# First attention: a quarter of each chunk's values done one step later, and the heads copied in one piece

## What is computed

```
h = layer_norm(x, ln1_g, ln1_b)
q, k, v = split(h @ w_qkv.T)                 # 16 heads of 16
# chunks of 128 queries; keys: the chunk before and the own one
scores = (q . kcat) / 4
scores = where((j >= i + 1) & (j <= i + 128) & valid, scores, -inf)
attn = softmax(scores)
x = x + (attn @ vcat) @ w_o.T
```

## Time and profile before

| | |
|---|---|
| median of 3 runs (lowest, highest) | 1763.08 us (1760.52, 1764.54) |
| the profiled execution | 1759.69 us |
| its span in the profile | 1757.9 us, and 1.8 us around it |
| PE, DVE, ACT, POOL busy | 96%, 82%, 67%, 60% |
| first attention | from the start to about 370 us |
| granted clock of PE from 40 to 370 us | 1.00 |

### The profile page before, as it was taken

How to read it: one execution, slowest core, us unless ns; L and a number is a source line. 1 busy time by engine, 2 the same in 40 slices (tenths; PEclk the granted TensorE clock), 3 DMA queues, 4 the chain that set the end, 5 groups by cost and what they waited for, 6 DMA issues and landing times.

```text
span 1757.9 us, 43282 instructions
## 1 busy us (share of the span) xinstructions
PE 1695.5 (96%) x15168; PEld 1460.7 (83%) x15168; DVE 1446.6 (82%) x3686; ACT 1170.4 (67%) x3024; POOL 1052.0 (60%) x1052
## 2 busy tenths in 40 slices
PE   6999999989999999999998999999999999999997
PEld 4777777779998788888887888878888888888886
DVE  6888988868887999989997655579999999967776
ACT  6999888855544778878775343367787787743332
POOL 3676566534334687887774444367878777634333
PEclk9999999999999999999999999999999999999999
DMA  3111211022322322222223313122222222131221
GB/s 109 38 38 38 65 38 35 26 103 66 117 72 65 98 81 66 76 76 66 80 67 89 107 54 99 54 92 75 80 63 81 72 70 81 56 111 60 73 84 37
DMA packets 174626, 125.44 MB, mean 71 GB/s; under 512 B 20824, under 2 KB 173664, under 8 KB 173664
## 3 DMA queue, kind: packets, MB, share of 16 engines
q1 hardware_dynamic: 174432, 122.98, 23.0%
HBM read 88.32 MB, written 34.61 MB: 70 GB/s over the span
## 4 chain that ended last, share of the span: by engine, by line
PE 84%; DVE 9%; ACT 3%; issue 3%; DMA 1%; POOL 0%; SPq 0%; POOLq 0%; DVEq 0%; ACTq 0%
PE psum L612 18%; PE psum L614 17%; PE psum L613 17%; PE psum L948 6%; PE psum L916 5%; PE psum L929 5%; PE psum L727 3%; PE psum L709 3%; PE psum L890 3%; ACT a_probs L1757 2%; PE psum L662 1%; DVE a_neg_max L1240 1%; DVE psum L1238 1%; PE psum L699 1%; PE psum L1053 1%
## 5 line engine op out<-in xcount | busy, mean ns | idle before, releaser
L1876 ACT ACTIVATE b_probs<-masked,neg_max 128x256 f32<-128x256 f32 (+1 forms) x512 | 249.8, 489 | 119.4 <-DVE neg_max L1370 119.4
L612 PE MATMUL psum<-wa_hi,b_h_hi 128*128 128x512 f32 (+1 forms) x576 | 234.4, 407 | 6.0 <-DVE wa_lo L1167 3.6
L614 PE MATMUL psum<-wa_hi,b_h_lo 128*128 128x512 f32 (+1 forms) x576 | 214.1, 372 | 0.0
L613 PE MATMUL psum<-wa_lo,b_h_hi 128*128 128x512 f32 (+1 forms) x576 | 214.0, 372 | 0.0
L1370 DVE CUSTOM_DVE_ANT_0 masked<-psum,mask 128x256 f32<-128x256 f32 (+1 forms) x512 | 177.2, 412 | 41.1 <-PE psum L916 40.2
L612 PE MATMUL psum<-g_h_hi,wm_hi 128*128 128x512 f32 (+1 forms) x480 | 190.3, 397 | 3.5 <-POOL g_h_lo L2148 2.4
L2105 POOL TENSOR_TENSOR g_in<-g_in,minus_half 128x16 f32<-128x16 f32 x64 | 187.7, 2933 | 5.3
L614 PE MATMUL psum<-g_h_hi,wm_lo 128*128 128x512 f32 (+1 forms) x480 | 189.2, 394 | 0.0
L613 PE MATMUL psum<-g_h_lo,wm_hi 128*128 128x512 f32 (+1 forms) x480 | 189.2, 394 | 0.0
L1962 ACT ACTIVATE gate<-psum,vec_b 128x512 f32<-128x512 f32 x96 | 66.0, 687 | 153.6 <-PE psum L614 153.5
L612 PE MATMUL psum<-wm_hi,u_hi 128*128 128x256 f32 x576 | 164.5, 286 | 0.1
(11 more groups left out here) (167 smaller groups left out, 5432.6 us busy)
## 6 DMA issues: line engine op xcount, KB each, us to landing
b_inv_t<-inverse_rows SPq DMA_DIRECT2D x128, 128.0 KB, 3.0
x_mid<-y_out SPq DMA_DIRECT2D x96, 128.0 KB, 2.3
rope_in<-in_rope SPq DMA_DIRECT2D x64, 128.0 KB, 2.4
x_res<-x_state SPq DMA_DIRECT2D x64, 128.0 KB, 2.8
g_in<-x_mid SPq DMA_DIRECT2D x32, 256.0 KB, 3.7
w_raw<-in_w_mlp_b SPq DMA_DIRECT2D x2, 2154.0 KB, 9.1
x_in<-in_x SPq DMA_DIRECT2D x32, 128.0 KB, 2.2
x_res<-in_x SPq DMA_DIRECT2D x32, 128.0 KB, 2.2
```

The costliest lines, as they stand in the source:

```text
L612: nc.tensor.matmul(out, a_hi, b_hi, start=first, stop=False)
L613: nc.tensor.matmul(out, a_hi, b_lo, start=False, stop=False)
L614: return nc.tensor.matmul(out, a_lo, b_hi, start=False, stop=last)
L1876: ins = nc.scalar.activation(out, src, ACT.Exp, bias=neg_max[:, r, k:k + 1], scale=-1.0, accum_out=row_sum[:, n % 2, 4 * r + k:4 * r + k + 1])
```

## The change

values takes a tuple of tiles in place of p. Tile 0 of chunk n stays in step n; tile 1 (a quarter of the chunk's values) moves to step n+1, between project_qk and transpose_probs(4(n+1)). The last chunk (n = 31) keeps tiles 0 and 1 together. Tiles 2 and 3 stay where they were, but no longer wait for head_copied. pv_done is still raised twice a chunk, after tile 1 and after tile 3. copy_heads copies all 512 columns in one instruction at the place of the former second copy, head_copied counts one per chunk, and the waits for it are renumbered.

```diff
--- before.py
+++ after.py
@@ -106,6 +106,16 @@
 ...
+
+
+def a_early_tiles(n):
+
+    return (0, 1) if n == NCH - 1 else (0,)
+
+
+def a_late_tiles(n):
+
+    return (1,)
 
 
 def a_heads_bank(n):
@@ -709,28 +719,28 @@
                     mm = nc.tensor.transpose(W2[:, k * P:k * P + P], a_probs[:, i % 2, k, :], ident[:])
                 mm.then_inc(S["pt_ready"], 1)
 
-            def values(n, p):
-
-
-                if n + p > 0:
-                    pe.wait_ge(S["head_copied"], 2 * n + p)
-                if p == 0:
+            def values(n, tiles):
+
+                p = tiles[0] // 2
+                if tiles[0] == 0:
+                    if n > 0:
+                        pe.wait_ge(S["head_copied"], n)
                     pe.wait_ge(S["v_copied"], n + 1)
                     if a_chunk(n - 2):
                         pe.wait_ge(S["y_ready"], min(n - 1, NCH - 3))
                 pe.wait_ge(S["select_ready"], 4 * n + 2 * p + 2)
                 blocks = [(n, p_now)] if a_batch_first(n) else [(n - 1, p_before), (n, p_now)]
-                for j in range(2):
-                    t = 2 * p + j
+                for t in tiles:
                     for m, probs_of in blocks:
                         for g in range(4):
                             mm = nc.tensor.matmul(O[32 * g:32 * g + 32, t * P:t * P + P], v_aug[:, m % VRING, 4 * t + g, :],
-                                                  probs_of[:, 2 * p + g // 2, 2 * (g % 2) + j, :],
+                                                  probs_of[:, 2 * p + g // 2, 2 * (g % 2) + t % 2, :],
                                                   start=(m == blocks[0][0]), stop=(m == n), tile_position=(0, 32 * g))
-                mm.then_inc(S["pv_done"], 1)
+                if tiles[-1] % 2 == 1:
+                    mm.then_inc(S["pv_done"], 1)
 
             def transpose_heads(n):
-                pe.wait_ge(S["head_copied"], 2 * n + 2)
+                pe.wait_ge(S["head_copied"], n + 1)
                 pe.wait_ge(S["qt_ready"], min(n + 3, NCH))
                 if 0 < n < NCH - 1:
                     pe.wait_ge(S["o_lo"], n)
@@ -752,7 +762,7 @@
                 pe.wait_ge(S["o_hi"], n + 1)
                 pe.wait_ge(S["o_lo"], n + 1)
                 if n < NCH - 3:
-                    pe.wait_ge(S["head_copied"], 2 * n + 4)
+                    pe.wait_ge(S["head_copied"], n + 2)
                 else:
                     pe.wait_ge(S["pt_copied"], 4 * NCH)
                 if n > NCH - 3:
@@ -782,10 +792,12 @@
                     transpose_z(s + 2)
                 if a_chunk(s + 1) and s > -1:
                     project_qk(s + 1)
+                if a_chunk(s - 1):
+                    values(s - 1, a_late_tiles(s - 1))
                 if a_chunk(s):
                     transpose_probs(4 * s)
                 if a_chunk(s - 1):
-                    values(s - 1, 1)
+                    values(s - 1, (2, 3))
                 if a_chunk(s):
                     scores(s, 1)
                     transpose_probs(4 * s + 1)
@@ -800,7 +812,7 @@
                     transpose_k(s + 1)
                 if a_chunk(s):
                     transpose_probs(4 * s + 2)
-                    values(s, 0)
+                    values(s, a_early_tiles(s))
                 if a_chunk(s - 1) and s < NCH - 1:
                     transpose_heads(s - 1)
 
@@ -808,7 +820,7 @@
             pe_mlp(pe, MLP_A, MA, None, opening=0)
             out_project(NCH - 3)
             transpose_heads(NCH - 2)
-            values(NCH - 1, 1)
+            values(NCH - 1, (2, 3))
             transpose_o(NCH - 2)
             pe_mlp(pe, MLP_A, MA, None, opening=1)
             transpose_heads(NCH - 1)
@@ -1766,12 +1778,11 @@
                     a.wait_ge(S["pv_done"], 2 * (n - 1) + r // 2 + 1)
                 nc.scalar.activation(p_now[:, r, :, :].rearrange("p h q -> p (h q)"), W2[:], ACT.Copy).then_inc(S["pt_copied"], 1)
 
-            def copy_heads(n, p):
-                a.wait_ge(S["pv_done"], 2 * n + p + 1)
+            def copy_heads(n):
+                a.wait_ge(S["pv_done"], 2 * n + 2)
                 if n > 0:
                     a.wait_ge(S["out_steps"], 3 * n - 2)
-                at = slice(p * D, p * D + D)
-                nc.scalar.activation(head_t[:, at], O[:, at], ACT.Copy).then_inc(S["head_copied"], 1)
+                nc.scalar.activation(head_t[:], O[:], ACT.Copy).then_inc(S["head_copied"], 1)
 
             def o_high(n):
                 a.wait_ge(S["out_steps"], a_out_step(n, 1))
@@ -1780,13 +1791,10 @@
 
             for s in a_steps():
                 if a_chunk(s - 1):
-                    if s < NCH:
-                        copy_heads(s - 1, 0)
                     copy_probs(4 * s - 1)
                     if s == NCH:
                         act_mlp(a, MLP_A, MA, None, opening="gate")
-                        copy_heads(s - 1, 0)
-                        copy_heads(s - 1, 1)
+                        copy_heads(s - 1)
                 if a_chunk(s - 2) and s != NCH - 1:
                     o_high(s - 2)
                 if a_chunk(s):
```

## The result

| | before | changed |
|---|---|---|
| median of 10 runs each | 1762.46 us | 1767.59 us (1765.25 to 1769.1) |
| profiled execution, its span | 1759.69, 1757.9 us | 1765.25, 1763.5 us |
| a steady step of the first attention | 10.79 us | 11.00 us |

The changed kernel is slower: the ratio is 1.0028, 95% interval [1.0018, 1.0038], or +5.1 us. The forecast was +6.1 us and 1769.2, on a base of 1763.1.

What follows compares the result with a forecast made beforehand. PE bounds the kernel, but in the first attention's steps ACT's exponentials hold the scores; +7.2 us over the steps and -1.1 at the tail give +6.1 on 1763.1, so 1769.2 us; 8 in 10: 1762.5 to 1772.5.

Steps and rivals of the forecast that it cites:

- this case: The whole kernel gets slower: chance 0.77, forecast 1769.2 us, own range 1768 to 1772 us with the spread of runs.
- the second rival: Late values between project_qk and transposes cost no switching: +0.02 us a step, 1762.5 us; 15% for within 0.2%.
- The wait that takes the place of the work: Before scores(s+1, 0): 0.44 us of removed PE work becomes waiting, since scores need ACT's exponentials + 0.14; gain 0.
- the ring: One first-attention step as a loop: PE to the heads' transposes, then DVE and ACT, back to PE; 10.79 us a turn.
- The heads held by q_t: End of a step: the heads' transposes wait for finish_q_t, as in step 16 (q_t ends 200.71, heads start 200.81).
- The price of the insertion: Last project_qk matmul to round 0's transposes: 0.93 us against 0.66 with late values, +0.27 us a step (+0.24 to +0.30).
- The sum over the steps: Late values in s = 1 to 31, 26 of these steps at the full 0.27 us: +7.2 us (6.4 to 8.1).
- The copy of the heads: On ACT: one 128x512 copy of 0.60 us replaces two of 0.46, growing by 0.14 ahead of copy_probs(4s+1); cost 0.
- the cover: ACT's idle time ahead of copy_probs(4s+1): 0.26 us, and 0.27 more since PE comes later, hiding the wider copy's growth.
- the third rival: Wider heads copy ends after copy_probs(4s+1) could start: up to 0.14 us in 29 steps, +4.1, 1773.3 us; 5%.
- The tail: At values(31, second half): the wait for the first half's heads copy is dropped, PE gains 1.08 us; -1.1 us.
- The first rival: ACT doesn't hold the scores, so PE keeps 0.44 us a step: -0.14 to -0.20 a step, 1757.4 us total; 7%.

## Why the prediction was right, point by point

**The total.** The way and the mechanism were right, the size was not quite. The change was forecast as +6.1 us, from 5.3 to 7.0, and cost 5.1, which is below that range; 1767.59 also lies below the 1768 to 1772 given for this case. It lies within 1762.5 to 1772.5, but that range was drawn down for the second rival, which did not come. Of the 1.6 us between 1769.2 and 1767.59, 1.0 is the change and 0.6 the base, since ten runs of the kernel before have a median of 1762.46 where three had 1763.08.

**The wait that takes the place of the work.** Right, to 0.02 us. The step that decided the sign was to ask how far ACT's exponentials ended ahead of the scores (0.15 in the step that was read, 0.14 in most), and how near they could come (0.14, rows 6). All profiles with ACT on the ring show 0.14 to 0.15.

**The heads held by q_t.** Right: heads start 0.10 after q_t's end in the changed kernel, as they did after step 16. It costs nothing, since the scores' wait is longer.

**The price of the insertion.** Taken as 0.93, with 0.90 and 0.96 as bounds; it is 0.89 to 0.90. The rule from the recorded end (values start 0.07 before the end of what precedes them) holds behind a 512-wide matmul too: 318.32 + 0.39 = 318.71, and the values start at 318.64. So my way in of 0.385 was too long, and the middle was the wrong choice: the late values start 0.32 behind the last matmul of project_qk, under the 0.33 to 0.39 that I had named as a sign. The spacings are 0.09 us longer on the way in (318.32 to 318.64, less the usual 0.235) and 0.10 us on the way out (0.33 from last group to transposes, less 0.23). The Trainium skill's "TensorEngine Tiling", section "Tiling Modes", says that a change of mode drains TensorE. The trace agrees in that time is lost at both changes; that it is a drain, and not something else in which these matmuls differ, no run here shows. The Trainium skill's "TensorE: Matmul & The Clock Gate", Part 2, says that weight loads are pulled ahead of matmuls in flight, if the row groups don't conflict or the load goes to the background buffer. Whether any were pulled ahead here isn't shown; the 0.09 and 0.10 us remained, so the second rival's condition wasn't met.

**The sum over the steps.** Forecast +7.2, from 6.4 to 8.1. Measured between the heads of s = 1 and of s = 30: 313.38 us before, 318.94 after, +5.6. This is the term that was mis-sized: it fell below its lower bound, by the price of the insertion above and by step 29. A steady step grew by 0.22, not 0.27: 0.235 for the insertion less 0.01 to 0.02 at the scores, which I had rounded to nothing. 25 such steps give 5.5; s = 16 and 17 together 0.14. Step 29 became shorter by 0.11 (11.54 to 11.43) where I had counted a full 0.27. There DVE has the MLP's first statistics to do and runs without a break from the merging of the step's first scores to the end of y_out, 331.75 to 340.63 before and 338.36 to 347.25 after: 8.88 and 8.89 us. The late values stand beside that run and cost nothing. Ahead of it 0.17 us is lost (DVE starts 1.56 after the heads of s = 28 instead of 1.39, since the scores there are held by ACT), and behind it 0.29 is gained (from y_out to the heads 0.98 instead of 1.27), since 8 matmuls are gone. In the kernel before the scores behind these heads stood 0.24 after ACT, so that ACT left room for this.

**The copy of the heads.** Right that it costs nothing, though it grew by 0.21 to 0.22 and not by 0.14. That is very near what the cover holds: in the kernel before it leaves 0.03 us, so there the third rival was closer than I wrote. In the changed kernel ACT still idles 0.27 us behind the wide copy, since its copy of the probabilities comes later with the insertion.

**The tail.** Right: from the transposes of round 0 in s = 31 to the last heads it is 13.88 us before and 12.74 after, -1.1.

**Balance.** In the two profiles: +0.8 at the heads of s = 1, +5.6 in steps 2 to 30, +0.2 from there to those transposes, -1.1 at the tail and +0.2 behind it; rounded, the 5.6 us of the spans. Of the 0.8, 0.9 lies ahead of anything that the change touches (the first transposes of round 2 start at 27.01 before and 27.94 after, both ahead of the first values), in the start-up. That is a spread of executions: the kernel with the heads in two copies has the same program up to there and starts its first values at 27.29, the changed one at 28.52, and the heads of s = 1 stand between 38.6 and 40.9 us in the kernels here. It happens to bring the +5.6 of this pair of profiles near the +6.1 that was forecast, which is luck: without it the change accounts for +4.5 us up to the last heads (370.60 before, 375.98 after, less the 0.93), and the medians say +5.1.

**The first rival**, ACT not holding the scores, wasn't wrong as arithmetic. Where ACT's run is shorter by two exponentials, the change gains 10.78 - 10.56 = 0.22 us a step (0.14 to 0.20 was written), and 5.3 us in the medians with the tail in them (1759.96 over ten runs against 1754.7 over four). The forecast turned on which bound holds, and in the real kernel that is ACT.

No version here that does all of the work beats the kernel before by what its time can show. The one with the heads copied at once, alone, is 1.1 us shorter in the tail of its profile and equal in the medians. Whether ACT's run can be shortened with all of its work done wasn't tried.

## What to carry to other kernels

Before work is moved from one side of a wait to the other, measure the slack on both sides: how long after its latest producer the consumer starts, against the shortest such distance seen at a place where PE is plainly waiting. A producer that ends just that long before means a wait of zero length, which the page doesn't show, and work taken out in front of it is worth nothing. The releaser that a view of waits names can be the wrong one, as k_t_low was here. A gap is only as wide as what it must hold with its switches: here 0.42 us of idle time took in 0.44 us of matmuls and still cost 0.22, 0.19 of it for the way in and out.

## What the runs showed of the hardware that I hadn't expected

The shortest distance from a producer's end to PE's start differed by what follows: 0.04 to 0.05 us from exponentials to the transposes of probabilities, and 0.14 to 0.15 from exponentials to the scores (32-row tiles). From k_t_low to the same scores it is at most 0.09 (once 0.06), for where that was seen PE's own spacing held them. Why the wait for ACT's four short instructions is the longer one isn't shown. Also, two copies of 128x256 back to back on ACT took 0.74 us and one of 128x512 took 0.67, though one of the halves by itself is recorded as 0.46: the second starts 0.27 us after the first.
